# First MoE stage of a fused four-stage kernel: weights split and chunks 0 and 1 prepared inside the preceding FFN, routing in four parts

## The reference

```python
x = x + 0.5 * ffn(layernorm(x))        # FFN 0: silu(x w1)*(x w2), gelu(. h1), gelu(. h2), . w3
x = x + mamba(layernorm(x))
x = x + 0.5 * ffn(layernorm(x))        # FFN 1, same weights
x = x + 0.5 * moe(layernorm(x))        # MoE 0: the stage that the change is about
x = x + attention(layernorm(x))
x = x + 0.5 * moe(layernorm(x))        # MoE 1, same weights

def moe(x):                            # 16 experts, top 4, inner size 64
    scores = sigmoid(x @ gate_w.T)
    idx = top_k(scores + gate_b, 4)
    w = scores[idx] / sum(scores[idx]) * 2.5
    y = sum over experts e of comb[:, e] * (silu(x w_gate_e) * (x w_up_e)) @ w2_e
    return y + (silu(x s_gate) * (x s_up)) @ s_w2          # shared expert
```

## Time and profile before

| | us |
|---|---|
| median of 3 runs | 1894.06 (1890.33 to 1895.96) |
| the profiled execution, its own time | 1891.39 |
| its span, first to last instruction | 1889.9 |
| TensorE busy in the span | 1781.0 (94%) |
| VectorE, ScalarE, GpSimd busy | 1330.9, 1150.2, 1172.7 |

### The profile page before, as it was taken

The page is one execution under the profiler, slowest core; times in us unless marked ns, Lnnn a source line. Parts: engine busy times, 40 slices in busy tenths (PEclk is TensorE's granted clock), DMA queues, the critical chain, the costliest instruction groups (busy, mean ns, idle before and its releaser), DMA issues. The chain is left out here.

```text
span 1889.9 us, 29839 instructions
## 1 busy us (share of the span) xinstructions
PE 1781.0 (94%) x11031; PEld 1211.9 (64%) x11031; DVE 1330.9 (70%) x2493; ACT 1150.2 (61%) x1715; POOL 1172.7 (62%) x660
## 2 busy tenths in 40 slices
PE   9998999888999897899999999999999999999888
PEld 5883444334786674577777777777777777765466
DVE  5627899996445764777777777777777777778676
ACT  5326777853435447676767676766766676653554
POOL 5551677874554452377776776777767777677354
PEclk9999999999999999999999999999999999999999
DMA  3000000000001003121222222121212121200100
GB/s 100 1 1 1 1 0 1 1 0 1 1 1 50 1 1 100 39 60 48 60 53 55 54 54 65 44 70 42 66 36 71 48 60 47 58 24 12 50 6 17
DMA packets 43664, 66.03 MB, mean 35 GB/s; under 512 B 24768, under 2 KB 26176, under 8 KB 43264
## 3 DMA queue, kind: packets, MB, share of 16 engines
q1 hardware_dynamic: 43056, 63.54, 12.9%
q10 hardware_dynamic: 432, 0.59, 0.1%
q0 software_dynamic: 32, 0.00, 0.0%
HBM read 29.05 MB, written 1.24 MB: 16 GB/s over the span
## 5 line engine op out<-in xcount | busy, mean ns | idle before, releaser
L2422 POOL TENSOR_TENSOR at_e_lo<-at_e,at_e_hi 128x1024 fp32r<-128x1024 f32 x256 | 613.0, 2395 | 300.8 <-DVE at_e_hi L2397 296.4
L2179 ACT ACTIVATE at_e<-at_ps,at_dropped 128x1024 f32<-128x1024 f32 x256 | 285.6, 1116 | 222.0 <-PE at_ps L1890 201.4
L2276 DVE CUSTOM_DVE_ANT_0 at_ps<-at_ps,at_mask 128x1024 f32<-128x1024 f32 x256 | 313.3, 1224 | 4.1 <-PE at_ps L2010 4.1
L2169 ACT ACTIVATE at_ps<-at_ps,at_neg_diag 128x1024 f32<-128x1024 f32 x256 | 278.6, 1088 | 36.7 <-DVE at_neg_diag L2267 36.4
L2397 DVE CAST at_e_hi<-at_e 128x1024 fp32r<-128x1024 f32 x256 | 233.8, 913 | 23.1 <-ACT at_e L2179 19.5
L1969 PE MATMUL at_ps<-at_kq,at_qk 64*128 64x512 f32 x768 | 221.0, 395 | 8.6 <-DMA at_kq<-at_qk 3.0
L2019 PE MATMUL at_ps<-at_qk,at_kq 64*128 64x512 f32 x768 | 224.7, 399 | 1.6 <-DVE at_row_max L2276 1.2
L1890 PE MATMUL at_pv_ps<-at_e_hi,at_v_hi 64*128 64x512 f32 x980 | 225.7, 453 | 0.2 <-issue 0.2
L2020 PE MATMUL at_ps<-at_kq,at_qk 64*128 64x512 f32 x768 | 224.8, 399 | 0.0
L1970 PE MATMUL at_ps<-at_qk,at_kq 64*128 64x512 f32 x768 | 221.1, 395 | 0.0
L1056 POOL TENSOR_TENSOR mb_work<-mb_work,mb_c 128x1024 f32<-128x1024 f32 x64 | 151.8, 2373 | 97.7 <-DVE mb_work L1025 97.6
(11 more groups left out here) (392 smaller groups left out, 4158.7 us busy)
## 6 DMA issues: line engine op xcount, KB each, us to landing
at_kq<-at_qk SPq DMA_DIRECT2D x128, 256.0 KB, 4.0
at_mask<-at_mask_dram SPq DMA_DIRECT2D x32, 256.0 KB, 3.6
at_recips<-at_recip_row SPq DMA_DIRECT2D x31, 256.0 KB, 4.4
ffn_h_raw<-in_h SPq DMA_DIRECT2D x2, 1024.0 KB, 7.6
at_head_w_raw<-in_w_qkv SPq DMA_DIRECT2D x32, 64.0 KB, 3.9
x<-in_x SPq DMA_DIRECT2D x4, 256.0 KB, 4.7
moe_gate_in<-in_gate_in SPq DMA_DIRECT2D x2, 512.0 KB, 3.9
moe_up_in<-in_up_in SPq DMA_DIRECT2D x2, 512.0 KB, 4.4
```

The source lines that it names most:

```text
L2169: act.eng.activation(ps[:], ps[:], ACT.Exp, scale=SCALE, bias=m.small["neg_diag"][s][:, blk:blk + 1], accum_out=m.small["sums"][s][:, blk: ...
L2179: act.eng.activation(m.e[e % 2][:], slot("turned_scores", h, blk)[:], ACT.Exp, scale=SCALE, bias=m.small["dropped"][h % SLOTS][:, blk:blk ...
L2276: dve.eng.tensor_tensor_reduce(out=ps[:], in0=ps[:], in1=m.mask[h % 2][:], scale=1.0, scalar=-BIG, op0=ALU.add, op1=ALU.max, accum_out=m.s ...
L2422: pool.eng.tensor_tensor(m.e_lo[e % 3][:], m.e[e % 2][:], m.e_hi[e % 3][:].bitcast(F32), ALU.subtract).then_inc(sem["at_lo"])
```

## The change

Weights and MoE working memory get fixed places, so that MoE 0's weights can be there while FFN 1 runs. The nine loads are issued when mamba's last chunk is done. `ffn` gets an argument `ahead`, which FFN 1 alone is given. In its first pair ScalarE and GpSimd split the MoE weights, one piece per slot (`AHEAD_SPLIT_HI`, `AHEAD_SPLIT_LO`; (layer, slot)), and GpSimd casts `pair_rows` and clears `comb`. In its second pair chunks 0 and 1 are normalized, rounded, scored, routed and turned. The mean of chunk 2 stands in the middle of the last chunk's w3 product. MoE 0 starts with `expert_in(0)` at once; it has no fills; chunks 2 and 3 are normalized between its first expert steps and scored at g = 5 and 6. In both stages `find_top` and `weigh` become four steps, one after each of p = 1 to 4 (in MoE 1's chunk 0: after 3, 3, 4, 5). `comb` and its transposed form hold two chunks instead of four.

```diff
+AHEAD_MEAN, AHEAD_VARIANCE, AHEAD_FINISH, AHEAD_ROUND, AHEAD_REST, AHEAD_LOGITS, AHEAD_SCORES = (
+    (0, 0), (0, 1), (0, 3), (0, 4), (0, 5), (0, 5), (0, 6))
+AHEAD_ROUTE = {(0, 7): ("top", 0), (1, 0): ("index", 0), (1, 1): ("hits", 0), (1, 2): ("weigh", 0),
+               (1, 3): ("top", 1), (1, 4): ("index", 1), (1, 5): ("hits", 1), (1, 6): ("weigh", 1)}
+AHEAD_TURN = {(1, 4): 0, (1, 7): 1}
+AHEAD_TURNED_IN = {(1, 5): 0, (2, 0): 1}
+AHEAD_SPLIT_HI = {(0, 2): 0, (0, 4): 1, (0, 6): 2, (1, 0): 3, (1, 1): 4}
+AHEAD_SPLIT_LO = {(0, 3): (0, 0), (0, 4): (0, 1), (0, 5): (1, 0), (0, 6): (1, 1), (0, 7): (2, 0), (1, 1): (2, 1),
+                  (1, 2): (3, None), (1, 3): (4, None)}
+AHEAD_PAIR_ROWS, AHEAD_CLEAR = (1, 4), (1, 6)
+MOE_STEPS = {1: ("top",), 2: ("index",), 3: ("hits",), 4: ("weigh",)}
+MOE_FIRST_STEPS = {3: ("top", "index"), 4: ("hits",), 5: ("weigh",)}
@@ ffn_pe, after each h1 and h2 slot of the second pair, and in w3
+                    if ahead and first:
+                        moe_ahead_pe(c, ahead, m_, (layer, slot))
...
+                if ahead and first and j and k == 1:
+                    pe.wait_ge(sem["x_ffn"], 2 * NCH - 1)
+                    pe.wait_ge(sem["moe_comb_lo"], MOE_AHEAD)
+                    norm_mean(pe, c, m_.norm_ps[0], c.x[:, COLS[MOE_AHEAD]])
@@ ffn_dve, after the last additions to x
+            if ahead and ch == MOE_AHEAD:
+                norm_centre(dve, c, 8 + ch, m_.norm_ps[0], c.x[:, COLS[ch]], ahead.xn[ch])
@@ moe_pe
-    logits(0)
-    fill_wait(pe, c, m.banks[3], 7)
-    expert_in(0)
-    expert_in(1)
-    logits(1)
-    logits(2)
-    fill_wait(pe, c, m.banks[6], 20)
-    turn(0)
...
+        if p == 0 and ch == 0 and t == 0:
+            pe.wait_ge(sem["norm_done"], 3 * (n0 + 2) + 1)
...
+    if t == 0:
+        expert_in(0)
+        pe.wait_ge(sem["x_ffn"], 2 * NCH)
+        norm_mean(pe, c, m.banks[1], c.x[:, COLS[3]])
+        norm_variance(pe, c, n0 + 2, m.banks[0], m.inv[2])
+        spread(0)
+        expert_in(1)
+        norm_variance(pe, c, n0 + 3, m.banks[1], m.inv[3])
+        spread(1)
...
+        if t == 0 and g == MOE_LATER_LOGITS:
+            for ch in range(2, NCH):
+                moe_logits(pe, c, m, t, ch, m.banks[1])
+MOE_LATER_LOGITS, MOE_LATER_ROUND, MOE_LATER_REST = 5, (4, 5), (5, 6)
+MOE_SCORES_AT = (6, 2)
@@ moe_act
+    if t == 0:
+        norm_square(act, c, n0 + 2, m.xn[2], m.inv[2])
+        silu(0)
+        norm_square(act, c, n0 + 3, m.xn[3], m.inv[3])
+        round_hidden(0)
+        silu(1)
+        round_hidden(1)
+        load_logs(act)
+        for ch in range(2, NCH):
+            norm_inverse(act, c, n0 + ch, m.banks[ch % 2], m.inv[ch], m.sq[ch])
@@ moe_dve
+    if t == 0:
+        norm_centre(dve, c, n0 + 3, m.banks[1], c.x[:, COLS[3]], m.xn[3])
+        for g in range(2):
+            weighed_product(g)
+        for ch in range(2, NCH):
+            finish(ch)
@@ build
             mamba(nc, c)
+            c.sp.wait_ge(c.sem["x_mamba"], NCH)
+            moe_load(nc, c, first_moe)
+            ffn(nc, c, 1, first_moe)
```

More of the change, by code:

```diff
@@ L321, in ffn_act, with ffn_dve @@
                         act.eng.activation(c.ffn_parts[k][0][:], m_.raw[k][:], ACT.Copy).then_inc(sem["ffn_w_hi"])
-    act.wait_ge(sem["x_ffn"], (t + 1) * NCH)
-def ffn_dve(c, m_, t):
+                    if ahead:
+                        moe_ahead_act(c, ahead, m_, first, (layer, slot))
+        if ahead and first:
+            moe_ahead_act(c, ahead, m_, first, (2, 0))
+    if not ahead:
+        act.wait_ge(sem["x_ffn"], (t + 1) * NCH)
+def ffn_dve(c, m_, t, ahead):
     dve, sem = c.dve, c.sem
@@ L393, in ffn_dve @@
                                               ALU.subtract).then_inc(sem["ffn_w_lo"])
+                    if ahead and first:
+                        moe_ahead_dve(c, ahead, m_, (layer, slot))
+        if ahead and first:
+            moe_ahead_dve(c, ahead, m_, (2, 0))
         for j in range(2):
@@ L1174, in moe_bank_free, with moe_bank @@
+MOE_TAKES = [moe_takes(t) for t in range(2)]
+MOE_TAKE_NO = [{key: k for k, key in enumerate(takes)} for takes in MOE_TAKES]
+def moe_bank(m, t, kind, g):
+    return m.ring[MOE_TAKE_NO[t][kind, g] % 6]
+def moe_bank_free(pe, c, t, kind, g):
+    take = MOE_TAKE_NO[t][kind, g] - 6
     g0 = t * MOE_G
     if take < 0:
-        if take >= -4:
+        if t == 0 and take >= -2:
+            pe.wait_ge(c.sem["x_ffn"], 2 * NCH)
+        elif t and take >= -4:
             pe.wait_ge(c.sem["norm_done"], 3 * (8 + 8 * t + take + 4) + 1)
@@ L1178, in moe_bank_free @@
         return
[L1179 to L1187, removed]
+    kind, g = MOE_TAKES[t][take]
     if kind == "gate":
@@ new lines, in moe_loaded, with moe_logits @@
+def moe_loaded(t, late=False):
+    n = len(MOE_LATE_LOADS if late else MOE_EARLY_LOADS)
+    return "moe_late_load" if late else "moe_load", 16 * n * (t + 1)
+def moe_logits(pe, c, m, t, ch, ps):
+    pe.wait_ge(c.sem["moe_load"], moe_loaded(t)[1])
+    pe.wait_ge(c.sem["norm_done"], 3 * (8 + 8 * t + ch) + 3)
+    for i in range(CT):
+        mm = pe.eng.matmul(ps[:, (ch * CT + i) * EXPERTS:(ch * CT + i + 1) * EXPERTS], m.xn[ch][:, i * P:(i + 1) * P],
+                           m.loads["gate_w"][:], start=True, stop=True)
+    mm.then_inc(c.sem["moe_logits"])
@@ new lines, in moe_ahead_dve @@
+def moe_ahead_dve(c, m, f, at):
+    dve = c.dve
+    if at == AHEAD_MEAN:
+        for ch in range(MOE_AHEAD):
+            norm_centre(dve, c, 8 + ch, f.norm_ps[ch], c.x[:, COLS[ch]], m.xn[ch])
+    if at == AHEAD_FINISH:
+        for ch in range(MOE_AHEAD):
+            norm_finish(dve, c, 8 + ch, f.norm_ps[ch], m.xn[ch], f.inv[ch], f.sq[ch])
+    if at in AHEAD_ROUTE:
+        step, ch = AHEAD_ROUTE[at]
+        moe_route(dve, c, m, 0, ch, step)
+    if at in AHEAD_TURNED_IN:
+        ch = AHEAD_TURNED_IN[at]
+        moe_rest_of_turned(dve, c, m, 0, ch, f.norm_ps[1 - ch])
@@ L1475, in moe_dve @@
+    for g in range(MOE_G):
+        ch, p = divmod(g, PAIRS + 1)
+        if g >= 2:
+            weighed_product(g)
+        if p == MOE_ADDED_AT and ch:
+            add_out(ch - 1)
+        for step in moe_steps_due(t, g):
+            moe_route(dve, c, m, t, ch + 1, step)
+        if p == MOE_TURNED_IN_AT and (1 if t else MOE_AHEAD) <= ch + 1 < NCH:
+            moe_rest_of_turned(dve, c, m, t, ch + 1, m.banks[(ch + 1) % 2])
     add_out(NCH - 1)
@@ L2561, in build @@
             c.mamba_loads = []
+            small_at = nc.sbuf_base
             c.ln_w = later("ln_w", [P, 1])
```

597 lines of the change are left out of this document (353 added, 244 removed).

## The result

The changed kernel takes **1875.32 us**, beside 1892.68 for the kernel before on the same chip; both are medians of four executions. One of the changed kernel's four (1873.0, 1874.35, 1876.3 and 1956.91) ran at a mean granted clock of 0.846 instead of 0.984 to 0.986, and without it the median is 1874.35. The ratio is 0.9908, with a 95% interval of 0.9894 to 0.9922: 17.4 us or 0.9% faster. The profiled execution took 1874.35 (span 1872.8), TensorE busy 95% of it.

A forecast was written before the change was run, and what follows sets the result against it. TensorE, 94% busy, was taken as the bound. Gains of 9.0 (56.6 - 38.8 - 8.8) and 2.9 sum to 11.9; 1891.39 less that is 1879.5, and 2.7 for the median gives 1882 us, range 1876 to 1889.

The forecast's parts named there:

- What FFN 1 pays: FFN 1 grows by 8.8 us (7 to 12): 7.0 of inserted TensorE work plus 1.8 of waits.
- rival B: In FFN 1, inserted steps delay casts and rests until TensorE waits in more slots: 8 us more, 1890; chance 0.10.
- The new start: MoE 0's start: one 5.1 us wait before the first `expert_out`; chunk 0 ends 38.8 after the FFN instead of 56.6.
- The 0.5 charged for the clock: MoE 0, behind the wait before the first `expert_out`: low clock costs 0.5 us (0 to 5), mostly hidden.
- the row: Table loads in MoE 0's start: trace row gives 1.28 us, chosen over the skill's 2.66, which would lengthen the wait by 2.8.
- Part 3: Routing in four steps gains 0.9 us in each of four routed chunks, 3.6; with MoE 1's chunk 0, 2.9 gained.
- MoE 1's chunk 0: `weigh` moves one product later, the turn waits 1.4 us longer and half comes back: -0.7 (-1.5 to 0).
- Nothing behind MoE 0 changes: Attention, behind MoE 0, was forecast to change by 0 us.
- Rival A: The clock stays low through MoE 0's new start, costing 4 to 5 us more: 1886 to 1887; chance 0.13.
- Rival D: Waits smaller than walked, logs issued sooner or routing wait gone altogether: 2 + 3 us more gained, 1877; chance 0.08.

The follow-up runs named there:

- the small subtractions: Changed kernel with routing back in two blocks and the GpSimd subtraction of pairs 2 to 4 of routed chunks cut to 64 of 512 columns: 1881.14 us, ratio 0.9939.
- the last kernel: Changed kernel with pair 2 before the norms, logits later, MoE 1's first routing in four parts, fills at several gaps including attention's norm: 1869.62 us, ratio 0.9885.

## Why the prediction was right or wrong

- **What FFN 1 pays: right.** 8.6 for 8.8, with the logits' wait 0.98 for 1.2, and 0.3 before the turn of chunk 1 for 0.5. (The waits listed there add up to 1.7, not 1.8.) That FFN 1 hides the work of the other engines held: TensorE had no other new wait over 0.2, and rival B did not come.
- **The new start: right in its mechanism, 1.5 too slow in size.** The one long wait sits where it was put and is released by the step named. It ends 12.0 after the FFN instead of 12.65, because rounding 1 ended at 7.8 and not at 8.4. The 0.5 charged for the clock was at most some 0.25, and the sigmoid's two table loads cost 1.24 instead of 2.15. The clock was low for over 5 us, not 3 to 4, and that was hidden. The load of the log table at 603.94 takes 1.28 and the next activation starts 0.02 behind its end. So the drain of about 1.38 that the Trainium skill adds to each switch ("ScalarE: Activation LUTs", What ACT_TABLE_LOAD costs) does not show here either, and the row was the right choice.
- **Part 3: the step that failed.** Its model was right for neighbouring blocks: about 0.98 of VectorE's time is free in a pair, lateness adds up, and some 1.4 is forgiven. With two blocks of 2.72 and 2.97, lateness reaches 3.7 and 2.3 should be lost; 2.2 was. With 1.58 and 2.01, beside the small subtractions, it gives 0.2; 0.4 and three times next to nothing was measured. The sizes put into it for the new order were wrong: 1.7, 1.7, 0.9 and 2.1 (sum 6.4) instead of 1.37, 0.98, 1.12 and 1.20 (4.7). I had taken the stretched durations of the earlier trace rows for the price of the steps. They are the price of the place: the same cast takes 0.18 where no GpSimd subtraction runs and 1.07 where it meets one. With the measured sizes lateness never passes 0.8, and nothing is lost. A smaller slip adds to it: by its own figures, 2.5 lost before and 1.4 after, the gain was 1.1 a chunk and not 0.9. That term was 3.6 and measured 8.7, 5.1 more. The trace's gain is 17.1 where the sum had 11.9, 5.2 more; all other differences (the start +1.5, before FFN 1 +0.9, MoE 1's lead-in +0.6, attention -2.9) nearly cancel.
- The Trainium skill states such a mechanism ("SBUF — State Buffer", Who interferes with whom): a VectorE instruction with two SBUF inputs contends with a GpSimd instruction that reads SBUF, for ports that the two engines share. One with at most one SBUF input does not, unless it runs in a 2-port mode, which a cast can enter. The runs agree: the two-input steps (bias addition 0.56 for 0.22, hits 1.08 for 0.42, multiplication 1.28 for 0.22) and the cast (1.06 for 0.17) stretch, while the products, which read PSUM (0.67 to 0.69), and the maxima and sums keep their durations in every trace. That it is the ports is the skill's reading; the runs show the stretch and that it goes with the subtraction.
- **MoE 1's chunk 0: right** (+0.7, the turn's wait 3.02 for the 3.1 forecast), but half told. The split did not free this chunk of the stretch, it moved it: the multiplication takes 0.22 here instead of 1.27, and the last two pieces of `weigh` 1.44 instead of 0.36, so that the product put ahead of `weigh` is paid in full. And the longer wait is more often followed by the low clock, 1.3 to 2.7 in six of nine traces. The two pieces in the changed kernel:

```profile
1794.94 1.44 DVE L1359 SCALAR_TENSOR_TENSOR moe_comb<-moe_biased,moe_total 128x64 f32<-128x64 f32 x2
```

- **"Nothing behind MoE 0 changes": wrong by 2.9 in the trace**, by the clock in front of attention. Rival A had the right suspect at the wrong place: it looked at the gap that the change makes, where other engines hid it, and not at short idle spots elsewhere, where nothing does.
- **The chances.** Rival D, with the routing waits gone altogether, had 0.08 and was nearest in time (1877) and, for the routing, in its reason. The bound of each term was kept (0 to 2.4 for the split), but the range joined the four routed chunks as if their errors would cancel. They are one error four times: at its upper bound, 9.6, that term alone moves 1882 to 1876, the end of the range, and nothing was left for the start.

## What to carry to other kernels

Price a small step by where it will stand, not by the mean of its durations: look for the same step with and without the other engine beside it, and see whether its end coincides with that engine's. A wait is where lateness surfaces, so before moving the step that a matmul waits for, ask which buffer or product was late first; a turn that waited 1.5 us was cured without gaining anything. And look for TensorE's short idle spots in front of long fp32 matmuls: where the clock fell behind them in front of attention it cost 1.5 to 2.9 us, and eight fills are a cheap try against it. Take more than one trace before you believe it.

## What the runs showed of the hardware

- The granted clock fell to 0.50 behind idle spots of only 1.17 and 0.78 us (changed kernel, 694 to 702), and stayed at 1.00 behind the same spots in other traces. Behind the turn's 3.01 to 3.03 it fell in six of nine traces; behind 1.78 to 1.80 it stayed up in three. In the last kernel it fell at 617 with no idle time over 0.42 in the 9 us before, behind the logits of chunks 2 and 3. So a low stretch belongs to the execution as much as to the kernel: attention, the same code in twelve traces, lasted 1051.1 to 1058.7 us in them, and the low clock at its start took 1.5 to 2.9 of that in six.
- A small VectorE step that is a cast or has two inputs in SBUF, and that meets a GpSimd subtraction under way, ended shortly behind it: the 128x16 cast 0.03 us, the 128x64 addition and multiplication 0.08, the 128x256 comparison 0.28. They took up to 1.28 instead of 0.17 to 0.42. Maxima, index searches and sums that met one were not stretched.
- Small bf16 matmuls in an idle spot cost the matmul behind them nothing where they ended before its wait did: the first `expert_out` starts 12.0 after the FFN without 18 fills and with them, and 20.5 lie between chunk 2's end and attention's first mean with and without eight. The clock was at 1.00 directly behind the filled spots in each of the traces that have them.
